# A decoder layer on one core: weighted values as eight 64x32 products side by side, with weights in places of their own

## What is computed

```python
x = layernorm(x + self_attention(x))       # linear attention, no softmax
q, k, v = heads(x @ W_q.T + b_q), heads(ctx @ W_k.T + b_k), heads(ctx @ W_v.T + b_v)   # 16 heads of 32, ctx[2, 154, 512]
scores = einsum('bhqd,bhkd->bhqk', q, k) / sqrt(32)
attn = softmax(where(Mask == 0, -1e9, scores))                     # over 154 keys
x = layernorm(x + einsum('bhqk,bhkd->bhqd', attn, v) @ W_o.T + b_o)
xr, xk = x_prev + mu_r * (x - x_prev), x_prev + mu_k * (x - x_prev)
x = layernorm(x + sigmoid(xr @ W_r.T) * (relu(xk @ W_k2.T) ** 2 @ W_v2.T))
```

## Time and profile before

| | us |
|---|---|
| median of three runs | 918.09 |
| span of the profiled execution | 916.3 |
| PE busy (matmuls) | 903.6, 99% |
| DVE busy | 715.3, 78% |
| ACT busy | 552.3, 60% |
| POOL busy | 507.2, 55% |

### The profile page before, as it was taken

The page is one execution under the profiler, slowest core; times in us unless marked ns, Lnnn a source line. Parts: engine busy times, 40 slices in busy tenths (PEclk is TensorE's granted clock), DMA queues, the critical chain, the costliest instruction groups (busy, mean ns, idle before and its releaser), DMA issues.

```text
span 916.3 us, 19065 instructions
## 1 busy us (share of the span) xinstructions
PE 903.6 (99%) x6726; PEld 735.5 (80%) x6726; DVE 715.3 (78%) x1994; ACT 552.3 (60%) x1667; POOL 507.2 (55%) x505
## 2 busy tenths in 40 slices
PE   8999999999999999999999999999999999999997
PEld 7867767777888888887878888888787878787876
DVE  7697566577887878797979788887878787879775
ACT  7455236857765656565757575756665757575631
POOL 1053015858684757575756657575666766656420
PEclk9999999999999999999999999999999999999999
DMA  8771020113010000002000000101010100100001
GB/s 300 240 248 49 27 91 9 35 43 127 9 47 9 30 26 24 31 24 89 24 31 24 31 24 24 31 25 31 24 30 25 31 25 14 41 2 24 2 24 46
DMA packets 31033, 45.65 MB, mean 50 GB/s; under 512 B 2779, under 2 KB 15579, under 8 KB 30811
## 3 DMA queue, kind: packets, MB, share of 16 engines
q1 hardware_dynamic: 27339, 37.36, 12.7%
q10 hardware_dynamic: 3600, 7.08, 2.2%
HBM read 34.10 MB, written 9.70 MB: 48 GB/s over the span
## 4 chain that ended last, share of the span: by engine, by line
PE 75%; DVE 5%; issue 3%; POOL 3%; ACT 1%; POOLq 0%; ACTq 0%
PE dense L88 18%; PE dense L90 17%; PE dense L89 17%; PE turned L1590 5%; PE scores L1578 4%; PE rest_value L1604 4%; PE rest_value L1608 3%; PE dense L1477 2%; PE turned L1477 1%; PE rest_value L1596 1%; POOL row_inv L1383 1%; POOL prob L1389 1%; PE scores L1483 1%; DVE prob L1112 1%; DVE stats L1071 1%
## 5 line engine op out<-in xcount | busy, mean ns | idle before, releaser
L1383 POOL TENSOR_TENSOR row_inv<-row_sum,minus_one 128x4 f32<-128x4 f32 x128 | 145.9, 1139 | 255.1 <-ACT prob L794 253.5
L794 ACT ACTIVATE prob<-prob,row_min 128x154 f32<-128x154 f32 x512 | 209.5, 417 | 17.8 <-DVE row_min L1112 17.8
L1389 POOL TENSOR_TENSOR prob<-prob,row_inv 128x512 f32<-128x512 f32 x128 | 142.1, 1110 | 0.0
L1112 DVE CUSTOM_DVE_ANT_0 prob<-scores,mask_add 128x154 f32<-128x154 f32 x512 | 127.1, 310 | 3.7 <-PE scores L1578 3.7
L802 ACT ACTIVATE prob_t<-turned 128x512 f32<-128x512 f32 x128 | 75.9, 593 | 57.5 <-PE turned L1590 57.4
L794 ACT ACTIVATION_READ_ACCUMULATOR prob<-prob,row_min 128x1 f32 x512 | 98.7, 193 | 0.0
L1590 PE MATMUL turned<-ident,prob 128*128 128x128 f32 x512 | 77.0, 273 | 1.3 <-ACT prob_t L802 0.8
L88 PE MATMUL dense<-xt_hi,cross_wq_hi 128*128 128x256 f32 x256 | 75.0, 293 | 0.5 <-DVE xt_lo L1103 0.5
L88 PE MATMUL dense<-mix_k_hi,ffn_wk_hi 128*128 128x256 f32 x256 | 74.5, 291 | 0.0
L1170 DVE TENSOR_TENSOR k_act_lo<-square,k_act_hi 128x512 fp32r<-128x512 f32 x32 | 50.3, 1573 | 28.2 <-ACT k_act_hi L827 28.2
L89 PE MATMUL dense<-xt_lo,cross_wq_hi 128*128 128x256 f32 x256 | 72.2, 282 | 0.0
(11 more groups left out here) (296 smaller groups left out, 2709.4 us busy)
## 6 DMA issues: line engine op xcount, KB each, us to landing
x_rows<-x_rows SPq DMA_DIRECT2D x32, 256.0 KB, 3.6
xt_raw<-x_cols SPq DMA_DIRECT2D x16, 512.0 KB, 3.7
out<-gate_then_y SPq DMA_DIRECT2D x15, 512.0 KB, 2.8
mask_in<-mask SPq DMA_DIRECT2D x16, 154.0 KB, 2.4
cross_wv<-cross_wv SPq DMA_DIRECT2D x2, 512.0 KB, 5.9
cross_wk<-cross_wk SPq DMA_DIRECT2D x1, 1024.0 KB, 8.7
self_wv<-self_wv ACTq DMA_DIRECT2D x1, 1024.0 KB, 7.6
self_wk<-self_wk ACTq DMA_DIRECT2D x1, 1024.0 KB, 12.0
```

The source lines that it names most:

```text
L794: m = act.activation(keys, keys, ACT.Exp, bias=row_min[:, buf, t, h:h + 1], scale=-1.0, accum_out=row_sum[:, buf, t, h:h + 1])
L1112: m = dve.tensor_tensor_reduce(prob[buf][:, t, h * CTX:(h + 1) * CTX], s_bank[:, h, t * CTX:(t + 1) * CTX], mask_add[n % 2][:, t, :], -SCA ...
L1383: pool.tensor_tensor(row_inv[:, buf, t, :], row_sum[:, buf, t, :], minus_one[:], ALU.pow).then_inc(*p_inv.up)
L1389: pool.tensor_tensor(keys[:, :, 0:P], keys[:, :, 0:P], inv.broadcast_to([P, HPG, P]), ALU.mult).then_inc(*p_norm.up)
```

## The change

Each head's products in `values` are cut in three pieces of keys (64, 64, 26), each with a stationary operand of 64 rows by 32 columns; head h of tile t uses the lower or upper 64 rows by `(h + t) % 2`, so that eight such products stand side by side. Heads' results for the two t go to two banks, one of which is the bank of the turns. `weigh` writes into a tile of its own, `weight`, with two places; `prob` has three places in a ring. The context's values stand twice in SBUF, once for each half of the rows (26 copies in place of 11). `diff` has no tile of its own any more. Turns and products are in another order on PE, and some products are cut in halves around turns (`early`, `late_half`, parts).

```diff
+EXP_SLOTS, WEIGHT_SLOTS = 3, 2
+SIDES = 2
+SIDE_ROWS = P // SIDES
+PIECES = P // SIDE_ROWS
+def side_of(h, t):
+    return (h + t) % SIDES
+def place_of(h, t):
+    return h // SIDES * SIDES + side_of(h, t)
...
+    for side in range(SIDES):
         for b in range(B):
+            for piece in range(PIECES):
+                row, end = b * CTX + piece * SIDE_ROWS, b * CTX + (piece + 1) * SIDE_ROWS
+                while row < end:
+                    n, to = min(end - row, P - row % P), side * SIDE_ROWS + row - end + SIDE_ROWS
+                    placements.append((v_first[to:to + n, b, piece, :], v_raw[row % P:row % P + n, row // P, :]))
+                    row += n
...
             def take_sums(b):
                 dve.wait_ge(*gram_mm.at((b + 1) * HALF - 1))
+                if b:
+                    dve.wait_ge(*placed.at(0))
...
-    rest_t, value = rv_bank[:, 0:GT], rv_bank[:, GT:2 * GT]
+    rest_t, value = rv_bank[:, 0:GT], psum[1][:, :, GT:GT + P]
...
+        end_diff = mem.over("prob", "end_diff", [P, KT, GT])
+        diff_of = lambda n: end_diff if n == LAST else mixed["r" if n == LAST - 1 else "k"]
...
             def load_mask(n):
-                if n:
-                    sp.wait_ge(*mask_ok.at(n - 1))
-                sp.dma_start(mask_in[:], io["mask"][n * GT:(n + 1) * GT, :]
+                if n >= 2:
+                    sp.wait_ge(*s_min.at(n - 2))
+                sp.dma_start(mask_in[n % 2][:], io["mask"][n * GT:(n + 1) * GT, :]
...
             def masked_min(n, g, t):
...
+                u = g * TPG + t
+                if n * UNITS + u >= EXP_SLOTS:
+                    dve.wait_ge(*p_norm.at(n, u + 1 - EXP_SLOTS))
...
             def difference(n):
                 dve.wait_ge(*x2t_out.at(n))
                 dve.wait_ge(*carried.at(n))
-                dve.tensor_tensor(diff[:], x2t[:, :, 1:1 + GT], x2t[:, :, 0:GT], ALU.subtract).then_inc(*diff_ok.up)
+                if n == LAST - 1:
+                    dve.wait_ge(*r_mm.at(n - 1))
+                elif 0 < n < LAST:
+                    dve.wait_ge(*k_mm.at(n - 1))
+                dve.tensor_tensor(diff_of(n)[:], x2t[:, :, 1:1 + GT], x2t[:, :, 0:GT], ALU.subtract).then_inc(*diff_ok.up)
...
+                if live(n):
+                    o_low(n, 2)
                 if live(f) and n > 1:
                     k_mix_low(f)
-                if live(n):
-                    o_low(n, 2)
...
             def weigh(n, g, t):
...
+                if n * UNITS + u >= WEIGHT_SLOTS:
+                    pool.wait_ge(*t_mm.at(n, u + 1 - WEIGHT_SLOTS))
+                pool.tensor_tensor(after, late, inv_late, ALU.mult)
+                pool.tensor_tensor(first, early, inv_early, ALU.mult).then_inc(*p_norm.up)
...
             def transposes(n, g, t):
                 u = g * TPG + t
                 pe.wait_ge(*p_norm.at(n, u + 1))
-                if n + u:
+                if t:
                     pe.wait_ge(*t_out.at(n, u))
-                if u == (2 * TPG - 1 if n == 1 else 2 * TPG) and 0 < n < LAST:
+                elif n + g:
+                    pe.wait_ge(*ot_lo_ok.at(n, g))
+                if u == 2 * TPG and 0 < n < LAST:
                     pe.wait_ge(*x2t_out.at(n - 1))
...
             def values(n, g):
                 pe.wait_ge(*t_out.at(n, (g + 1) * TPG))
                 pe.wait_ge(*rest_out.at(n, g + 1))
+                if g == 1 and 0 < n < LAST:
+                    pe.wait_ge(*x2t_out.at(n - 1, 1))
                 b = batch(n)
+                for piece in range(PIECES + 1):
+                    for t in range(TPG):
+                        for h in range(HPG):
+                            rows = slice(side_of(h, t) * SIDE_ROWS, (side_of(h, t) + 1) * SIDE_ROWS)
+                            cols = slice((g * HPG + h) * DK, (g * HPG + h + 1) * DK)
+                            if piece < PIECES:
+                                sta, block = v_first[rows, b, piece, cols], piece * PIECES + h // SIDES
+                            else:
+                                sta, block = v_rest[rows, b, g, h * DK:(h + 1) * DK], HPG
+                            m = pe.matmul(value[h * DK:(h + 1) * DK, t, :], sta, pt[rows, block, t * P:(t + 1) * P],
+                                          start=(piece == 0), stop=(piece == PIECES), skip_group_check=True)
```

More of the change, by code:

```diff
@@ L569, in main_tiles @@
     tile["q"] = mem.place("q", [P, HG, GT])
-    for i in range(2):
-        tile[f"prob{i}"] = mem.place(f"prob{i}", [P, TPG, GK])
+    tile["prob"] = mem.place("prob", [P, EXP_SLOTS, GK])
+    tile["weight"] = mem.place("weight", [P, WEIGHT_SLOTS, HPG * P])
     for i in range(2):
@@ new lines, in act_program @@
+            take_turned(0, 1, 1)
+            take_rest(0, 1)
+            x1t_high(1, 0)
+            x1t_high(1, 1)
+            o_high(0, 1)
+            exponentials(0, 2, 1)
+            take_turned(0, 2, 0)
+            exponentials(0, 3, 0)
+            take_q(1, 0)
+            u_high(0, 1)
+            take_turned(0, 2, 1)
+            take_rest(0, 2)
+            u_high(2, 3)
+            take_q(1, 1)
+            exponentials(0, 3, 1)
+            o_high(0, 2)
+            take_turned(0, 3, 0)
@@ new lines, in act_program @@
+            take_rest(1, 1)
+            take_m(2)
+            turned_x2(0, 0)
+            x1t_high(2, 0)
+            x1t_high(2, 1)
+            o_high(1, 1)
+            exponentials(1, 2, 1)
+            turned_x2(0, 1)
+            exponentials(1, 3, 0)
+            take_turned(1, 2, 0)
+            take_q(2, 0)
+            take_turned(1, 2, 1)
+            take_rest(1, 2)
+            exponentials(1, 3, 1)
+            take_q(2, 1)
+            mix_high(0, "r")
+            o_high(1, 2)
@@ new lines, in pe_program @@
+            early, late_half = range(KT // 2), range(KT // 2, KT)
+            for t in range(TPG):
+                y_product(0, t)
+            fold_t(1)
+            for t in range(TPG):
+                x1_turn(0, t)
+            fold_t(2)
+            for h in range(2):
+                q_product(0, h)
+            scores(0, 0)
+            fold_t(3)
+            scores(0, 1)
+            fold_kv()
+            transposes(0, 0, 0)
+            y_product(1, 0)
+            transposes(0, 0, 1)
@@ new lines, in pe_program @@
+            y_product(1, 1)
+            values(0, 0)
+            scores(0, 2)
+            fold_u(0, 1)
+            transposes(0, 1, 0)
+            fold_u(2, 3)
+            transposes(0, 1, 1)
+            x1_turn(1, 0)
+            x1_turn(1, 1)
+            values(0, 1)
+            scores(0, 3)
+            q_product(1, 0)
+            transposes(0, 2, 0)
+            q_product(1, 1, (0,))
+            transposes(0, 2, 1)
+            q_product(1, 1, (1,))
+            values(0, 2)
+            scores(1, 0)
```

567 lines of the change are left out of this document (271 added, 296 removed).

## The result

The changed kernel takes 988.02 us (median of 4 runs, 984.75 to 992.03), the kernel before 918.20 beside it: a ratio of 1.0759, 95% interval 1.0731 to 1.0786. That is slower, as forecast, but by 70 us instead of 37, and above the range. The profiled execution has a span of 990.1 us, 73.8 more than before.

The account below looks back on a forecast made before the run. The prediction took PE's queue (TensorE matmuls, 99% of the span) as the bound, unless waits enter it. Kernel before 918.1 + 38.1 for 13 groups - 1 outside them = 955 us; range 903 to 963.

Parts of the forecast that it names:

- T: Clock origin of the prediction's steps: the start of the third head group's first turn in a group of 256 queries.
- all outside the groups: Twelve more values calls -2.5 us, prologue copies +1, the wait at the end about 0.6: sum -1 us.
- The chain: `difference` waits for k_product; DVE's queue and POOL collisions delay q_product and v_product: +2.93 us a group, +38.1 over 13.
- rival 5: PE's clock falls in the 2.9 us gap before v_product: +38 us, 993 us; chance 0.04.
- that new wait: Turns newly wait for `o_low` on PE; taken as hidden and priced at nothing, 0.1-0.2 us a group without cover.
- The values: Each values call on PE falls from 1.01 to 0.79-0.80 us, 64 times: a gain of 13.4 us.
- rival 4: In values, the 48 starts or row halves hold each other up: call 1.45 us, time 997 us; chance 0.05.
- The turns moved: Reordered turns on PE change shape-change costs by -0.1 to +0.3 us a group, taken as +0.1.
- Rivals 1 to 3: Port collides once: 946 us, 0.20; v_product's cover holds: 907, 0.27; stalls of 0.7 us a group eat the gain: 918, 0.06.

Follow-up runs that it names:

- filler_in_the_gap: The changed kernel with twelve dummy matmuls on PE just ahead of v_product(e, 0)'s wait for `k_act_lo`: 968.15 us, 1.0541.
- and_last_o_low_first: and_x2_turn_earlier with, in the last group, `o_low(LAST, 2)` ahead of `v_finish(LAST - 2, 0)` on DVE: 917.99 us, 0.9994.
- and_x2_turn_earlier: diff_in_spare_bytes plus POOL's `r_mix_low` waiting for `k_low(e, 1)`, and `x2_turn(f, 1)` back ahead of both halves of `k_product(e, 1)`: 920.79 us, 1.0024.
- diff_in_spare_bytes: The changed kernel with `difference` writing into unused halves of `ot_hi` and `ot_lo`, its wait for k_product removed: 935.91 us, 1.0193.

## Why the prediction was wrong

Step by step, in T, for the group shown above:

| step of the prediction | forecast | measured |
|---|---|---|
| turn (0, 0) to T | 26.98 | 27.03 |
| a call of values | 0.79-0.80 | 0.87 |
| `difference` | 0.22-1.44 | 0.30-1.52 |
| blend r ends | 3.98 | 4.02 |
| q_product(a, 1) starts | 4.65 | 4.76 |
| k blends end | 11.3 | 11.24 |
| `k_low` ends | 12.05 | 12.11 |
| v_product(e, 0) starts | 12.1 | 12.16 |
| from there to the next first turn | 11.35 | 12.99; 11.42 at full clock |
| a group | 50.43 | 52.18; 52.79 on average; 50.62 at full clock |
| all outside the groups | -1 | +6.1 |

**The chain was right.** Both rows of blends, `k_square` and `k_low` end within 0.1 us of the forecast, single blends within about 0.2. The steady groups at full clock take 50.62 where the prediction has 50.43. That the wait makes this and that the port makes most of it were shown by taking each away (935.9 and 931.8) and by adding the wait to the other kernel (967.2).

**The step that failed is rival 5, the clock.** In the profiled execution, 36.7 us over its forecast of 953.4, it is 24.2 (filler_in_the_gap). The prediction gave it 0.04, with the reason "No row shows such a gap". It should have been a term of the sum: the forecast itself made the gap of nearly 3 us, so the only question was what the clock does in one. And a row of before did answer that, at the very end, where PE has finished and DVE still works (windows of the kernel before, columns as above):

```profile
909.00:910.00 1.00, 0.73 (x7) 0.53 (x5) 0.90 (x5) 0.00 (x0) 0.41 (x1) 1.00 0.00 0
...
911.00:912.00 1.00, 0.00 (x0) 0.00 (x0) 0.93 (x3) 0.00 (x0) 0.00 (x0) 1.00 0.00 0
912.00:913.00 1.00, 0.00 (x0) 0.00 (x0) 0.84 (x4) 0.00 (x0) 0.47 (x1) 0.52 0.00 0
```

PE's last matmul ends at 909.7, and from about 912 the clock is at its lower level: 2.3 us without work were enough there. With that row the sum would have been 955 plus up to 2.9 a group, 993 at most, and the range would have held the result. The row says that the clock can fall in such a gap, and not how often: in the other 13 traces the same fall comes 2.6 to 4.9 us after PE's last matmul, and one of the late ones, read alone, would have spoken for a clock that stays up. The rival's price was a bound and it was sound: the fall costs 0 to 2.9 us a group, 1.9 on average.

**The clock is not the whole miss.** With the clock kept up the kernel takes 968 us (filler_in_the_gap), which is still 13 over the forecast and 5 above the range. In the profiled execution 12.5 us are left beside the clock: 7.1 outside the groups, and 5.4 in the 13 groups (662.0 - 618.5 = 43.5 where the prediction has 38.1). Of these 5.4, the 0.19 a steady group is 2.5; the rounds n = 2, 6 and 7 hold the rest, 1.5 of it a turn at the end of n = 6 that waits for `o_low`, which the prediction had priced at nothing.

**Outside the groups** the forecast has -1 and the profiles +6.1. Of these, 2.4 are one wait of the last group's turn (3, 0) for `o_low`, shown by and_last_o_low_first; the prediction had looked at that new wait in the steady groups only. Another 2.5 us lie ahead of the round n = 2, 1.8 of them in the round n = 0, where PE waits for `u` and for the remainder's turn; the one try at them failed. They and the last 1.2 us at the end stay open.

**The values** were off by 0.07 us a call, 4.5 us in all if every call is on the chain. The six rounds of eight tiles came at 0.11 us as forecast; the filling and change of shape around them is 0.87 - 0.66 = 0.21 instead of 0.13. The 48 starts hold nothing up, and rival 4 is out. 0.87 us for 48 records is 18 ns each. That is below the 25 ns that the Trainium skill gives as the least distance (TensorE: Matmul & The Clock Gate, "Wait — 56ns, not 53.3ns?"); for matmuls in different tiles the measurement decides.

**The turns moved** were priced for PE alone, and that price was right (26.98 against 27.03). Their effect on DVE was left out: the x2 turn in the middle of k_product makes `difference` 0.8 us later (T-0.33 against T-1.10). In the changed kernel the new wait covers this. Without the wait it shows, and was worth 3.2 us.

Rivals 1 to 3 fell with the DVE rows: POOL's instructions stand among both blends. What the change was worth without its side effects can be read off and_x2_turn_earlier: a group of 47.01 us against 47.50, the 46.76 of the prediction plus 4 x 0.07 for the values. That would be 6.4 us over 13 groups. The rounds 2 and 6 take 2.9 of it back (the 13 groups fall by 3.5, from 618.5 to 615.0), and the start and the end take the rest and 2.4 us more.

## What to carry to other kernels

Where a forecast opens a gap on TensorE, the clock after it belongs in the sum and not among the rivals: the end of the kernel's own trace, where TensorE is done and others work on, shows that it can fall, though one such end doesn't show how often. A tile saved by writing into another's bytes costs what stands in the queue behind the new wait, then what the delayed instructions now collide with, then what the clock does in the gap; here the three were 0.9, 2.8 and 1.9 us a group, and the last two went away with one wait on the other engine. "Hidden" holds only beside the schedule it was worked out for: the turn's wait for `o_low` was hidden while v_product was late, and cost 3.2 us a group as soon as it was on time.

## What was not expected of the hardware

- A wait more on POOL made the kernel 56 us faster (988.0 to 931.8 us), since four two-operand instructions of DVE ran in 2.46 us instead of 6.70, and with the gap the fall of the clock went too.
- The carry copy, 128x4 elements with one operand, takes 0.17 us alone and 2.16 us when it is issued in POOL's `r_mix_low` (diff_in_spare_bytes). So not only DVE's two-operand instructions are held.
- The clock fell in 12 of 13 groups at gaps of 2.7 us, in 5 of 13 at 2.1, and in 5 of 21 gaps of 1.6 to 1.8 us over all traces; one group kept it at 2.7. Gaps of up to 1.4 us never cost it (0 of 38). The changed kernel's runs spread over 7 us, those of before over 1.1; that the number of groups in which the clock falls makes this spread was not tried.
